# Layer 3's row scales of a four-layer GNN stack, made wholly on GpSimd instead of on VectorE and GpSimd

## The chip, the cores and the metric

The kernel runs on one core of a Trainium2 chip. The metric is the device time of one launch in microseconds (us). Engine names in the profile: PE is TensorE (matmul), PEld its weight loads, DVE is VectorE, ACT is ScalarE, POOL is GpSimd, SP is SyncE, which issues the output DMAs.

## The reference, cut to what matters

Four residual layers run over a batch of 128 graphs of 128 nodes with 64 features: `x = x + layer(relu(layernorm(x)))`, each with its own graph network. The change lies where layer 2's output is folded into `x` and layer 3 begins.

```python
def _layernorm(x, axis=-1, eps=1e-5):
    m = jnp.mean(x, axis=axis, keepdims=True)
    v = jnp.var(x, axis=axis, keepdims=True)
    return (x - m) / jnp.sqrt(v + eps)
...
# end of layer 2: y is normalised over all nodes, then
y = ((y - mean) / jnp.sqrt(var + BN_EPS) * gamma + beta) * m
return jax.nn.relu(y)
...
# layer 3
h = jnp.maximum(_layernorm(x, axis=-1), 0.0)
messages = jnp.einsum('bij,bjh->bih', adjacency, h)
node_in = jnp.concatenate([h, messages], axis=-1)
dh = jnp.tanh(node_in @ W1 + b1) @ W2 + b2
x = x + dh
```

What the change touches is the layernorm of layer 3: for each node and graph, the inverse root of its variance (`rstd`) and the negative mean times it (`nmr`).

## The kernel before, in words

Nodes lie on the 128 partitions and graphs with their features on the free axis, so `x_all` and `y` (a part of `work`) are 128 x 8192 in float32 and stay in SBUF. Layer 0 is the long part of the run (about the first 1000 us), then layer 1 (to about 1220 us), layer 2 (to about 1277 us), and a block that begins with layer 2's batch normalisation (to about 1322 us). The last piece of that block, from about 1322 us to the end, is the fold: layer 2's result is added to `x` while layer 3 already runs over it. The change lies only there.

**Chunks.** The fold cuts `y` and `x` into NXC = 16 chunks of 8 graphs (128 x 512). For each chunk VectorE multiplies `y` by a row vector (`scale_chunk`, L1472), GpSimd adds `beta` (`shift_chunk`, L1477, called the shift below), ScalarE applies the masked relu graph by graph (`masked_relu`, L1599, eight activations in two halves), and VectorE adds it to `x` (L1483) and takes `bn_stats` of each of the eight graphs (L280, both in `add_to_x`).

**Batches.** The layernorm scales are made for QC = 3 chunks at a time, 24 columns; there are NB = 6 batches, the last of one chunk (8 columns). For each batch VectorE makes the variances (`variances`, L1498 to L1506, six instructions), GpSimd raises them to the power of minus a half (L1534), and VectorE corrects that estimate by one Newton step and makes `nmr` (`scales`, L1514 to L1520, four instructions). ScalarE waits for `nmr` of a batch before it normalises the first graphs of it (`norm_group`).

**Layer 3.** It runs over NI = 16 iterations i of two units u = 0 and 1, each of four graphs; a unit is written (i, u) below. Iteration i covers the eight graphs of chunk i. ScalarE normalises four graphs (L1146, `norm_group`, one iteration ahead), TensorE multiplies by the adjacency and transposes (`neighbours`, L1662 and L1666), VectorE copies the sums out of PSUM (L1552, `copy_sums`), TensorE makes the hidden layer (`hidden`, L1672 and L1673), ScalarE the tanh (L1622), TensorE the product (`product`, L1681), VectorE adds the bias to `x` and then the product (L1557 and L1562, `update`), and SP stores the result.

**Order.** Every engine's order is written out by hand. VectorE in iteration i: copy (i, 1), update (i-1, 1), `add_to_x` of chunk i+5, scales of a batch if it is their turn, variances of a batch if its last chunk has just been added, copy (i+1, 0), update (i, 0), `scale_chunk` of chunk i+8. ScalarE in iteration i, unit u: `norm_group` (i+1, u), tanh (i, u), half of the masked relu of chunk i+6. TensorE in iteration i: neighbours (i, 1), hidden (i, 0), product (i-1, 1), neighbours (i+1, 0), hidden (i, 1), product (i, 0). GpSimd: shifts 0 to 4, the power of batch 0, shifts 5 to 7, then for each batch k from 1 its power and the shifts 3k+5 to 3k+7, as far as there are chunks. Five chunks are added before layer 3's first copy, so that batch 0 (chunks 0 to 2) is made ahead of the loop, and the last chunk of batch k is added in iteration 3k-3. Batch k's `nmr` is first read in ScalarE's iteration 3k-1.

Of the kernel before, what the change touches and what calls it, by code (L numbers as in the profile page):

```python
# [7 lines left out]
ALU = mybir.AluOpType  # L8
# [4 lines left out]
def gnn_stack_kernel(nc, a, out):  # L13
# [12 lines left out]
    B, N, F = a["x"].shape  # L26
# [15 lines left out]
    EPS = 1e-5  # L42
    KEY = 257.0
    XC = 512
    NXC = B * F // XC
# [3 lines left out]
    with ctx:  # L49
        def sb(name, shape, dt=F32):  # L50
            return ctx.enter_context(nc.sbuf_tensor(name, shape, dt))

        def sem(name):
            return ctx.enter_context(nc.semaphore(name))
# [52 lines left out]
        var = sb("var", [N, B])  # L107
        dif = sb("dif", [N, B])
        msum = sb("msum", [N, B])
        std = sb("std", [N, B])  # L110
        rstd = sb("rstd", [N, B])
        nmr = sb("nmr", [N, B])
# [1038 lines left out]
        def grp(u, i):  # L1151
            return 2 * i + u
# [280 lines left out]
        s_bn2 = sem("layer3_stats_made")  # L1433
# [9 lines left out]
        s_lnq = sem("l3_scales_step")  # L1443
        s_ln3 = sem("l3_scales_ready")
        s_minus = sem("minus_half_set")
        s_root = sem("inverse_root_estimated")
        LEAD = 6
        QC = 3
        NB = (NXC + QC - 1) // QC
        minus_half = sb("minus_half", [N, QC * GX])  # L1450
# [19 lines left out]
        def scale_chunk(c):  # L1470

            nc.vector.tensor_tensor(g3(yc(c)), g3(yc(c)), per_feature(stat[:, 5, :]), ALU.mult).then_inc(s_ya, 1)  # L1472

        def shift_chunk(pool, c):

            pool.wait_ge(s_ya, c + 1)
            nc.gpsimd.tensor_tensor(g3(yc(c)), g3(yc(c)), per_feature(beta[:, :]), ALU.add).then_inc(s_yb, 1)  # L1477

        def add_to_x(dve, c):

            v = nc.vector
            dve.wait_ge(s_yc, 2 * c + 2)
            v.tensor_tensor(xc(c), xc(c), yc(c), ALU.add).then_inc(s_xn, 1)  # L1483
            dve.wait_ge(s_xn, c + 1)
            for e in range(GX):
                last = stats(c * GX + e)
            last.then_inc(s_bn2, 1)

        def batch(k):
            return slice(k * QC * GX, min((k + 1) * QC, NXC) * GX)  # L1490

        def variances(dve, k):

            v = nc.vector
            cols = batch(k)
            m0, q0, m1, q1 = (bn6[:, cols, t] for t in (1, 2, 4, 5))
            dve.wait_ge(s_bn2, min(QC * k + QC, NXC))
            v.tensor_tensor(msum[:, cols], m0, m1, ALU.add)  # L1498
            v.tensor_tensor(var[:, cols], q0, q1, ALU.add)
            v.tensor_tensor(dif[:, cols], m0, m1, ALU.subtract).then_inc(s_lnq, 1)  # L1500
            dve.wait_ge(s_lnq, 6 * k + 1)
            v.tensor_scalar(var[:, cols], var[:, cols], 1.0 / F, EPS, ALU.mult, ALU.add)
            v.scalar_tensor_tensor(out=dif[:, cols], in0=dif[:, cols], scalar=0.25, in1=dif[:, cols],
                                   op0=ALU.mult, op1=ALU.mult).then_inc(s_lnq, 1)
            dve.wait_ge(s_lnq, 6 * k + 2)
            v.tensor_tensor(var[:, cols], var[:, cols], dif[:, cols], ALU.add).then_inc(s_lnq, 1)  # L1506

        def scales(dve, k):

            v = nc.vector  # L1510
            cols = batch(k)
            root, error = std[:, cols], dif[:, cols]
            dve.wait_ge(s_root, k + 1)
            v.scalar_tensor_tensor(out=error, in0=root, scalar=-0.5, in1=root, op0=ALU.mult, op1=ALU.mult)             .then_inc(s_lnq, 1)  # L1514
            dve.wait_ge(s_lnq, 6 * k + 4)
            v.tensor_tensor(error, error, var[:, cols], ALU.mult).then_inc(s_lnq, 1)
            dve.wait_ge(s_lnq, 6 * k + 5)
            v.scalar_tensor_tensor(out=rstd[:, cols], in0=error, scalar=1.5, in1=root, op0=ALU.add, op1=ALU.mult)             .then_inc(s_lnq, 1)
            dve.wait_ge(s_lnq, 6 * k + 6)
            v.scalar_tensor_tensor(out=nmr[:, cols], in0=msum[:, cols], scalar=-0.5, in1=rstd[:, cols],  # L1520
                                   op0=ALU.mult, op1=ALU.mult).then_inc(s_ln3, 1)

        def shifts_and_roots(pool):

            g = nc.gpsimd

            def shifts(first, past):
                for c in range(first, past):
                    shift_chunk(pool, c)

            def inverse_root(k):
                cols = batch(k)
                pool.wait_ge(s_lnq, 6 * k + 3)
                g.tensor_tensor(std[:, cols], var[:, cols], minus_half[:, 0:cols.stop - cols.start], ALU.pow)\  # L1534
                 .then_inc(s_root, 1)

            g.memset(minus_half[:, :], -0.5).then_inc(s_minus, 1)
            pool.wait_ge(s_minus, 1)
            shifts(0, LEAD - 1)
            inverse_root(0)  # L1540
            shifts(LEAD - 1, LEAD + 2)
            for k in range(1, NB):
                inverse_root(k)
                shifts(min(QC * k + LEAD - 1, NXC), min(QC * k + QC + LEAD - 1, NXC))

        def fold_in(dve):

            v = nc.vector

            def copy_sums(i, u):  # L1550
                dve.wait_ge(s_agg3[u], i + 1)
                v.tensor_copy(msg[:, u, :], bank[4 * u][:, :]).then_inc(s_aggs3[u], 1)  # L1552

            def update(i, u):
                if i > 0:
                    dve.wait_ge(s_out[u], 16 * i)
                v.tensor_tensor(upd[:, u, :].rearrange("p (q f) -> p q f", q=GS),  # L1557
                                x[:, ds(GS * grp(u, i) * F, GS * F)].rearrange("p (q f) -> p q f", q=GS),
                                l3b2[:, :].unsqueeze(1).broadcast_to([N, GS, F]), ALU.add).then_inc(s_xb[u], 1)
                dve.wait_ge(s_dh[u], i + 1)  # L1560
                dve.wait_ge(s_xb[u], i + 1)
                v.tensor_tensor(upd[:, u, :], bank[4 * u + 2][:, 0:GS * F], upd[:, u, :], ALU.add)\  # L1562
                 .then_inc(s_new[u], 1)

            for c in range(3):
                scale_chunk(c)
            for c in range(LEAD - 1):
                add_to_x(dve, c)
                if c == QC - 1:
                    variances(dve, 0)  # L1570
                if c + 3 <= LEAD + 1:
                    scale_chunk(c + 3)
            scales(dve, 0)
            copy_sums(0, 0)
            for i in range(NI):
                copy_sums(i, 1)
                if i > 0:
                    update(i - 1, 1)
                if i + LEAD - 1 < NXC:
                    add_to_x(dve, i + LEAD - 1)  # L1580
                if (i + 2) % QC == 0 and (i + 2) // QC < NB:
                    scales(dve, (i + 2) // QC)
                last = i + LEAD - 1
                if last == NXC - 1 or (last < NXC and last % QC == QC - 1):
                    variances(dve, last // QC)
                if i + 1 < NI:
                    copy_sums(i + 1, 0)
                update(i, 0)
                if i + LEAD + 2 < NXC:
                    scale_chunk(i + LEAD + 2)  # L1590
            update(NI - 1, 1)
# [47 lines left out]
        with nc.Block() as block:  # L1639
# [102 lines left out]
            @block.gpsimd  # L1742
            def _(pool):
                g = nc.gpsimd

                g.memset(block_mask, 1.0).then_inc(s_cutmask, 1)
                pool.wait_ge(s_cutmask, 1)
                g.affine_select(out=block_mask, in_=block_mask, compare_op=ALU.is_ge, fill=0.0,
                                base=0, pattern=[[1, XC]], channel_multiplier=-F).then_inc(s_cutmask, 1)
                pool.wait_ge(s_cutmask, 2)  # L1750
                g.affine_select(out=block_mask, in_=block_mask, compare_op=ALU.is_ge, fill=0.0,
                                base=F - 1, pattern=[[-1, XC]], channel_multiplier=F).then_inc(s_cutmask, 1)
                pool.wait_ge(s_vb, 2)
                normalise(pool, g, 1)
                pool.wait_ge(s_mean, 1)
                centre(pool, g, 1)
                shifts_and_roots(pool)

            @block.sync
            def _(sp):  # L1760
# [34 lines left out]
```

## Time and profile before

| | |
|---|---|
| median of 3 runs | 1448.39 us (1444.45 to 1448.88) |
| profiled execution, its own time | 1445.43 us |
| its span | 1443.7 us, so 1.7 us lie outside |
| PE busy | 1321.2 us (92%) |
| DVE busy | 1162.4 us (81%) |
| ACT busy | 1100.8 us (76%) |
| POOL busy | 510.4 us (35%) |
| mean granted TensorE clock | 0.977 |

The times in the rows are counted from the start of the span. The shares are means over five different stages; only the last 122 us of the span hold work that the change touches.

### The profile page before, as it was taken

What the parts mean: (1) busy time and instruction counts of PE and PEld (TensorE: products, weight loads), DVE (VectorE), ACT (ScalarE), POOL (GpSimd) and SP (SyncE); (2) the same over time, 40 slices, a digit from 0 to 9 for tenths busy, and PEclk for the clock granted to TensorE, in tenths of its full rate; (3) what the DMA queues carried; (4) which work ended last, traced back from release to release, by engine and by line L of the source; (5) the groups of instructions that cost most, each with busy time, mean ns of one, the idle gap of its engine ahead of it and who ended that gap; (6) DMA issues with size and microseconds to landing.
All of it is one profiled execution on the core that took longest, in us unless ns stands there. A gap on an engine that the chain in (4) does not pass through costs nothing. (4 is left out here: it accounts for less than half of the span.)

```text
span 1443.7 us, 40799 instructions
## 1 busy us (share of the span) xinstructions
PE 1321.2 (92%) x11243; PEld 1076.3 (75%) x11244; DVE 1162.4 (81%) x2949; ACT 1100.8 (76%) x2427; POOL 510.4 (35%) x610
## 2 busy tenths in 40 slices
PE   3999999999999999999999999997999998974688
PEld 1777778777787777787777877776988897930677
DVE  8898998889988898888988889886444454977896
ACT  4788888888888888888888888874555554925785
POOL 1333444434444334444344443432212221035441
PEclk9999999999999999999999999999999998987799
DMA  7000000000000000000000000000000000000012
GB/s 154 21 13 9 8 7 14 7 7 7 7 15 7 7 7 7 15 7 7 7 7 15 7 7 7 0 2 1 0 0 0 0 0 0 0 1 0 20 43 55
DMA packets 40928, 18.13 MB, mean 13 GB/s; under 512 B 19573, under 2 KB 40887, under 8 KB 40887
## 3 DMA queue, kind: packets, MB, share of 16 engines
q1 hardware_dynamic: 40354, 17.42, 4.9%
q8 instruction: 19, 0.31, 0.1%
q10 hardware_dynamic: 532, 0.21, 0.1%
q14 instruction: 23, 0.18, 0.0%
HBM read 13.44 MB, written 4.19 MB: 12 GB/s over the span
## 5 line engine op out<-in xcount | busy, mean ns | idle before, releaser
L724 DVE SCALAR_TENSOR_TENSOR acc<-slot_banks,acc 128x768 f32<-128x768 f32 x512 | 487.7, 952 | 77.5 <-PE slot_banks L443 68.3
L793 POOL TENSOR_TENSOR acc<-acc 128x384 f32<-128x384 f32 x128 | 128.0, 1000 | 529.6 <-DVE onediff L718 423.8
L443 PE MATMUL slot_banks<-ac_hi,work 128*128 128x192 f16 x1408 | 265.1, 247 | 27.6 <-DVE work L706 26.7
L443 PE MATMUL slot_banks<-ac_lo,work 128*128 128x192 f16 x1408 | 263.9, 246 | 0.0
L443 PEld LDWEIGHTS slot_banks<-ac_hi,work 128*128 (+1 forms) x1408 | 137.2, 97 | 98.8 <-issue 76.7
L443 PE MATMUL slot_banks<-ac_hi,onediff 128*128 128x192 f16 x1024 | 183.1, 246 | 6.9 <-DVE acc L724 5.1
L443 PE MATMUL slot_banks<-ac_lo,onediff 128*128 128x192 f16 x1024 | 182.4, 246 | 0.0
L443 PEld LDWEIGHTS slot_banks<-ac_lo,work 128*128 (+1 forms) x1408 | 138.0, 98 | 20.3 <-issue 14.5
L779 POOL TENSOR_TENSOR ac_lo<-ac,ac_hi 128x384 f16<-128x384 f32 x128 | 122.7, 959 | 49.4 <-ACT ac_hi L583 49.4
L543 ACT ACTIVATE work<-bank 128x512 f16<-128x512 f32 x256 | 130.5, 601 | 1.2 <-PE bank L354 1.2
L706 DVE TENSOR_SCALAR work<-work,slot_key 128x1024 f16 x256 | 118.0, 480 | 12.3 <-issue 3.7
L582 ACT ACTIVATE ac<-bank 128x384 f32<-128x384 f32 x128 | 62.1, 486 | 81.0 <-PE bank L403 81.0
L591 ACT ACTIVATE acc<-ac,neg_pad 128x768 f32<-128x768 f32 x128 | 119.3, 932 | 0.0
L443 PEld LDWEIGHTS slot_banks<-ac_hi,onediff 128*128 x1024 | 104.7, 102 | 17.1 <-issue 15.3
L607 ACT ACTIVATE slot_banks<-ac 128x768 f32<-128x768 f32 x127 | 103.5, 815 | 11.6
L403 PE MATMUL bank<-wac,hT 65*128 65x384 f32 x256 | 109.5, 510 | 1.7 <-ACT ac_hi L583 1.1
L600 ACT ACTIVATE work<-slot_banks 128x576 f32<-128x576 f32 x128 | 83.3, 651 | 34.9 <-PE slot_banks L443 33.3
L1146 ACT ACTIVATE onediff<-x_all,nmr,rstd 128x64 f32<-128x64 f32 (+1 forms) x256 | 90.7, 430 | 17.8 <-DVE nmr L1520 9.7
L1227 POOL TENSOR_TENSOR adjT_all<-adjT_all,ident 128x512 f32 x32 | 39.9, 1268 | 173.8 <-PE slot_banks L1179 173.8
L443 PEld LDWEIGHTS slot_banks<-ac_lo,onediff 128*128 x1024 | 100.3, 98 | 0.0
L718 DVE TENSOR_TENSOR onediff<-work x128 | 88.6, 692 | 7.4 <-DVE work L706 0.6
L436 PE MATMUL slot_banks<-ac_hi,ident 128*128 128x384 f16 x258 | 85.1, 330 | 0.9 <-issue 0.7
(272 smaller groups left out, 3311.0 us busy)
## 6 DMA issues: line engine op xcount, KB each, us to landing
adj_in<-in_adj_dram SPq DMA_DIRECT2D x32, 256.0 KB, 2.8
out_dram<-acc SPq DMA_DIRECT2D x32, 128.0 KB, 2.0
l1w<-in_L_gnn_W_dram SPq DMA_DIRECT2D x2, 64.0 KB
l1b<-in_L_gnn_b_dram SPq DMA_DIRECT2D x2, 64.0 KB
x_all<-in_x_dram SPq DMA_DIRECT2D x4, 0.2 KB, 11.7
nm_in<-in_nodemask_dram ACTq DMA_DIRECT2D x1, 64.0 KB
w1a<-in_L_gnn_W_dram ACTq DMA_DIRECT2D x1, 48.0 KB
w1b<-in_L_gnn_W_dram ACTq DMA_DIRECT2D x1, 48.0 KB
```

The source lines that it names most:

```text
L403: nc.tensor.matmul(pAC[:, 0:2 * H], hT0[:, p, q * N:(q + 1) * N], wac[:, :], start=True, stop=True)\
L436: nc.tensor.matmul(unit(pair, t, n), node, part[:, q, 0:H].unsqueeze(1).broadcast_to([N, n, H]), start=(e == 0), stop=False)
L443: last = nc.tensor.matmul(unit(pair, t, 1), hot(t), part[:, q, H:2 * H].unsqueeze(1), start=False, stop=(e == 1 and (t % SB == SB - 1 or t ...
L543: last = nc.scalar.activation(rs[:, p, :, t, :], pA3[:, :].rearrange("p (q j) -> p q j", q=GS), ACT.Copy, bias=-float(t))
L591: nc.scalar.activation(acc[:, q, :].rearrange("p (t h) -> p t h", t=SU), ac32[:, q, 0:H].unsqueeze(1).broadcast_to([N, SU, H]), ACT.Relu, ...
L607: nc.scalar.activation(unit((q + 1) % 2, 0, SU), ac32[:, q, 0:H].unsqueeze(1).broadcast_to([N, SU, H]), ACT.Copy).then_inc(s_seed, 1)
L706: nc.vector.tensor_scalar(onehot[:, ds(at, CH)], ranks.rearrange("p t j -> p (t j)"), slot_key[:, ds(key, 1)], None, ALU.is_equal).then_in ...
L718: nc.vector.tensor_tensor(onediff[:, ds(at, CH)], onehot[:, ds(at, CH)], onehot[:, ds(at_old, CH)], ALU.subtract).then_inc(s_D, 1)
L724: nc.vector.scalar_tensor_tensor(out=sums, in0=unit((q + k) % 2, 0, SU), scalar=0.0, in1=sums, op0=ALU.min, op1=ALU.add).then_inc(s_free[k ...
L779: nc.gpsimd.tensor_tensor(ac_lo[:, q, :], ac32[:, q, :], ac_hi[:, q, :], ALU.subtract)\
L793: nc.gpsimd.tensor_tensor(acc[:, q, 0:2 * H], acc[:, q, 0:2 * H], acc[:, q, 2 * H:4 * H], ALU.add)
L1146: ins = nc.scalar.activation(hn[:, u, SLOT[q] * F:(SLOT[q] + 1) * F], x[:, ds((b + q) * F, F)], ACT.Relu, bias=nmr[:, ds(b + q, 1)], scale ...
```

## The change

VectorE no longer makes variances and scales. GpSimd makes all of it in one chain, in the place in its order where the power stood: it waits for the statistics of the batch's last chunk, and issues 14 instructions instead of one, in ten steps with a semaphore wait between them. The correction is written without three-operand instructions, which is why ten VectorE instructions become thirteen on GpSimd beside the power. The shifts keep their places behind it.

```diff
-        def variances(dve, k):
...
-        def scales(dve, k):
...
+        def scales(pool, k):
+
+            g = nc.gpsimd
             cols = batch(k)
+            count = cols.stop - cols.start
             m0, q0, m1, q1 = (bn6[:, cols, t] for t in (1, 2, 4, 5))
             root, error = std[:, cols], dif[:, cols]
+            pool.wait_ge(s_bn2, min(QC * k + QC, NXC))
+            g.tensor_tensor(error, m0, m1, ALU.subtract)
+            g.tensor_tensor(var[:, cols], q0, q1, ALU.add)
+            g.tensor_tensor(msum[:, cols], m0, m1, ALU.add).then_inc(s_lnq, 1)
+            pool.wait_ge(s_lnq, 8 * k + 1)
+            g.tensor_tensor(error, error, error, ALU.mult)
+            g.tensor_scalar(var[:, cols], var[:, cols], 1.0 / F, EPS, ALU.mult, ALU.add)
+            g.tensor_scalar(msum[:, cols], msum[:, cols], -0.5, None, ALU.mult).then_inc(s_lnq, 1)
+            pool.wait_ge(s_lnq, 8 * k + 2)
+            g.tensor_scalar(error, error, 0.25, None, ALU.mult).then_inc(s_lnq, 1)
+            pool.wait_ge(s_lnq, 8 * k + 3)
+            g.tensor_tensor(var[:, cols], var[:, cols], error, ALU.add).then_inc(s_lnq, 1)
+            pool.wait_ge(s_lnq, 8 * k + 4)
+            g.tensor_tensor(root, var[:, cols], minus_half[:, 0:count], ALU.pow).then_inc(s_lnq, 1)
+            pool.wait_ge(s_lnq, 8 * k + 5)
+            g.tensor_tensor(error, root, root, ALU.mult).then_inc(s_lnq, 1)
+            pool.wait_ge(s_lnq, 8 * k + 6)
+            g.tensor_tensor(error, error, var[:, cols], ALU.mult).then_inc(s_lnq, 1)
+            pool.wait_ge(s_lnq, 8 * k + 7)
+            g.tensor_scalar(error, error, -0.5, 1.5, ALU.mult, ALU.add).then_inc(s_lnq, 1)
+            pool.wait_ge(s_lnq, 8 * k + 8)
+            g.tensor_tensor(rstd[:, cols], root, error, ALU.mult).then_inc(s_rs3, 1)
+            pool.wait_ge(s_rs3, k + 1)
+            g.tensor_tensor(nmr[:, cols], msum[:, cols], rstd[:, cols], ALU.mult).then_inc(s_ln3, 1)
...
             shifts(0, LEAD - 1)
-            inverse_root(0)
+            scales(pool, 0)
             shifts(LEAD - 1, LEAD + 2)
             for k in range(1, NB):
-                inverse_root(k)
+                scales(pool, k)
                 shifts(min(QC * k + LEAD - 1, NXC), min(QC * k + QC + LEAD - 1, NXC))
...
             for c in range(LEAD - 1):
                 add_to_x(dve, c)
-                if c == QC - 1:
-                    variances(dve, 0)
                 if c + 3 <= LEAD + 1:
                     scale_chunk(c + 3)
-            scales(dve, 0)
             copy_sums(0, 0)
...
                 if i + LEAD - 1 < NXC:
                     add_to_x(dve, i + LEAD - 1)
-                if (i + 2) % QC == 0 and (i + 2) // QC < NB:
-                    scales(dve, (i + 2) // QC)
-                last = i + LEAD - 1
-                if last == NXC - 1 or (last < NXC and last % QC == QC - 1):
-                    variances(dve, last // QC)
```

## Rows read from the trace of the kernel before

**Rows 1.** Windows: stretch and length; busy PE, PEld, DVE, ACT, POOL; clock; DMA
```profile
1372.00:1391.10 19.10, 16.12 (x110) 14.21 (x108) 18.15 (x58) 16.29 (x55) 7.96 (x4) 1.00 0.19 42
1418.00:1437.60 19.60, 19.60 (x147) 18.75 (x146) 12.51 (x30) 13.27 (x37) 0.00 (x0) 1.00 0.27 60
```

**Rows 2.** Chain of work that ended last: where it leaves VectorE
```profile
1416.60 0.70 PE slot_banks L1672 x2
```

**Rows 3.** VectorE timeline, head: start us, us, line, operation, output and inputs
```profile
1333.02 1.11 DVE L280 BATCH_NORM_STATS2 bn<-x_all 128x6 f32<-128x64 f32 x8
...
1340.35 1.28 DVE L1514 SCALAR_TENSOR_TENSOR dif<-std 128x24 f32<-128x24 f32 x1
...
1344.10 0.18 DVE L1520 SCALAR_TENSOR_TENSOR nmr<-msum,rstd 128x24 f32<-128x24 f32 x1
```

**Rows 4.** VectorE timeline, from batch 1's last chunk to batch 4's
```profile
1351.79 1.11 DVE L280 BATCH_NORM_STATS2 bn<-x_all 128x6 f32<-128x64 f32 x8
...
1370.88 1.11 DVE L280 BATCH_NORM_STATS2 bn<-x_all 128x6 f32<-128x64 f32 x8
1372.02 0.20 DVE L1498 TENSOR_TENSOR msum<-bn 128x24 f32<-128x24 f32 x1
...
1372.88 0.68 DVE L1552 COPY adj_in<-slot_banks 128x512 f32<-128x512 f32 x1
1373.47 0.41 DVE L1557 TENSOR_TENSOR acc<-x_all,l3b 128x256 f32<-128x256 f32 x1
...
1378.14 0.34 DVE L1514 SCALAR_TENSOR_TENSOR dif<-std 128x24 f32<-128x24 f32 x1
...
1379.06 0.68 DVE L1552 COPY adj_in<-slot_banks 128x512 f32<-128x512 f32 x1
...
1381.71 1.12 DVE L1557 TENSOR_TENSOR acc<-x_all,l3b 128x256 f32<-128x256 f32 x1
...
1389.97 1.11 DVE L280 BATCH_NORM_STATS2 bn<-x_all 128x6 f32<-128x64 f32 x8
...
1407.73 1.11 DVE L280 BATCH_NORM_STATS2 bn<-x_all 128x6 f32<-128x64 f32 x8
```

**Rows 5.** ScalarE timeline: norm groups of four graphs, and what they waited for
```profile
1352.80 1.42 ACT L1146 ACTIVATE onediff<-x_all,nmr,rstd 128x64 f32<-128x64 f32 x4
...
1355.43 1.44 ACT L1146 ACTIVATE onediff<-x_all,nmr,rstd 128x64 f32<-128x64 f32 x4
...
1379.23 1.43 ACT L1146 ACTIVATE onediff<-x_all,nmr,rstd 128x64 f32<-128x64 f32 x4 [0.39 <-DVE nmr L1520]
```

**Rows 6.** GpSimd timeline: powers of 24 and 8 columns, and one shift
```profile
1335.19 4.60 POOL L1534 TENSOR_TENSOR std<-var,minus_half 128x24 f32<-128x24 f32 x1 [1.08 <-DVE var L1506]
...
1373.04 4.17 POOL L1534 TENSOR_TENSOR std<-var,minus_half 128x24 f32<-128x24 f32 x1 [3.61 <-DVE var L1506]
...
1381.28 1.28 POOL L1477 TENSOR_TENSOR work<-work,beta 128x512 f32<-128x512 f32 x1 [2.83 <-DVE work L1472]
...
1416.02 1.64 POOL L1534 TENSOR_TENSOR std<-var,minus_half 128x8 f32<-128x8 f32 x1 [1.94 <-DVE var L1506]
```

**Rows 7.** GpSimd groups by shape: count, busy us, mean ns, idle us before
```profile
L793 POOL TENSOR_TENSOR acc<-acc 128x384 f32<-128x384 f32 x128 | 128.0, 1000 | 529.6 <-DVE onediff L718 423.8 <-ACT work L600 105.8
...
L797 POOL TENSOR_TENSOR hm<-work 128x192 f32<-128x192 f32 x128 | 76.9, 601 | 10.0
L795 POOL TENSOR_TENSOR work<-work 128x192 f32<-128x192 f32 x128 | 75.9, 593 | 0.0
...
L1537 POOL MEMSET minus_half<- 128x24 f32 x1 | 0.1, 117 | 0.0
```

**Rows 8.** TensorE timeline, iteration 11: neighbours (12, 0), product, next neighbours
```profile
1418.01 1.06 PE L1662 MATMUL slot_banks<-adjT_all,onediff 128*128 x8
...
1419.99 0.61 PE L1681 MATMUL slot_banks<-l3w,acc 128*128 128x128 f32 x4
1420.43 1.06 PE L1662 MATMUL bank<-adjT_all,onediff 128*128 x8
```

More of the change, by code:

```diff
@@ L1445, in gnn_stack_kernel @@
         s_minus = sem("minus_half_set")
-        s_root = sem("inverse_root_estimated")
+        s_rs3 = sem("l3_inverse_roots_ready")
         LEAD = 6
@@ L1490, in batch @@
             return slice(k * QC * GX, min((k + 1) * QC, NXC) * GX)
-        def variances(dve, k):
-            v = nc.vector
+        def scales(pool, k):
+            g = nc.gpsimd
             cols = batch(k)
+            count = cols.stop - cols.start
             m0, q0, m1, q1 = (bn6[:, cols, t] for t in (1, 2, 4, 5))
[L1497 to L1506, printed above, removed]
@@ L1508, in scales @@
-        def scales(dve, k):
-            v = nc.vector
-            cols = batch(k)
-            root, error = std[:, cols], dif[:, cols]
[L1513 to L1521, printed above, removed]
@@ L1523, in shifts_and_roots @@
-        def shifts_and_roots(pool):
+            root, error = std[:, cols], dif[:, cols]
+            pool.wait_ge(s_bn2, min(QC * k + QC, NXC))
[5 more added lines that the diff above has]
+            g.tensor_scalar(var[:, cols], var[:, cols], 1.0 / F, EPS, ALU.mult, ALU.add)
@@ L1525, in shifts_and_roots, with shifts_and_scales @@
+            pool.wait_ge(s_rs3, k + 1)
+            g.tensor_tensor(nmr[:, cols], msum[:, cols], rstd[:, cols], ALU.mult).then_inc(s_ln3, 1)
+        def shifts_and_scales(pool):
             g = nc.gpsimd
@@ L1529, in shifts @@
                     shift_chunk(pool, c)
[L1531 to L1535, printed above, removed]
             g.memset(minus_half[:, :], -0.5).then_inc(s_minus, 1)
@@ L1756, in _ @@
                 centre(pool, g, 1)
-                shifts_and_roots(pool)
+                shifts_and_scales(pool)
             @block.sync
```

## The prediction

> **What bounds the kernel now.** I read the windows of the fold first, to see which engine fills each stretch. While chunks are still being added, VectorE is busy 18.15 of 19.10 us, ahead of ScalarE (16.29) and TensorE (16.12). Once the chunks are done, TensorE fills 19.60 of 19.60 us and VectorE has a third of its time free [rows 1]. The chain of waits agrees: it runs down VectorE alone for some 60 us and changes to TensorE at 1416.60 [rows 2]. So only what VectorE does before that point can be worth time, and what it does behind it is free.
>
> The VectorE timeline gives the rhythm. I call T(k) the end of `bn_stats` of batch k's last chunk (start plus duration), where the batch's scales can begin: 1333.02 + 1.11 = 1334.13 for batch 0 [rows 3], then 1352.90, 1371.99, 1391.08 and 1408.84 [rows 4]. The periods are 19.09, 19.09 and 17.76 us. N(k) is the end of `nmr`. N(0) is 1344.28 [rows 3], so L(0) = N(0) - T(0) = 10.15 us; for batch 2, ScalarE waits 0.39 us for `nmr` and starts at 1379.23, so L(2) is about 7.1 us [rows 5]. `nmr` is already slightly late before the change. That is why I treat this as a question of latency as much as of work.
>
> **What is removed.** Per batch, variances take VectorE from 1371.99 to the next copy at 1372.88, 0.89 us, and scales from 1378.14 to 1379.06, 0.9 us [rows 4]. Ten instructions, 1.8 us per batch with issue gaps. The scales of batch 0 lie ahead of the loop where ScalarE waits for them, those of batch 5 behind 1416.60 where VectorE has time. VectorE's floor for a period becomes 19.09 - 1.8 = 17.3 us, of which 1.4 us is something else: twice per period L1557 takes 1.12 instead of 0.41 us (1381.71, five such in the fold) [rows 4], each time with a shift of 1.28 us running on GpSimd, that one from 1381.28 to 1382.56 [rows 6]. No DMA is issued or moved; SP's queue still waits on the same updates.
>
> **What is added.** Per batch GpSimd gets 13 instructions of 24 columns beside the power. The trace has no such instruction. Two groups of the same operation give a line: 1.000 us for 384 columns, 0.593 for 192, so 2.12 ns a column and 0.19 us fixed, 0.235 us at 24 columns [rows 7]. Bounds: below, the memset of 24 columns, 0.117 us, which reads nothing [rows 7]; above, the power, which took 4.17 us for 24 and 1.64 for 8 columns [rows 6], so 0.37 us fixed, and 0.42 us with 24 columns at 2.12 ns. I take 0.235, since it is the same kind of instruction, and keep both ends. A wait for GpSimd's own last result costs 10.0 us / 128 = 0.08 us (L797 follows L795 in that way) [rows 7].
>
> The chain undisturbed: 0.09 to start; two steps of three instructions, 2 x (0.2 + 0.2 + 0.235 + 0.08) = 1.43; two single steps, 2 x 0.315 = 0.63; the power, 4.17 + 0.08; four steps, 1.26; the last, 0.235. Sum 7.9 us. On top comes VectorE. The power of batch 0 took 4.60 instead of 4.17 us, started at 1335.19 beside a two-input VectorE instruction [rows 6], so a GpSimd instruction can wait for such a one. In a batch's first 3 us VectorE runs L1557 and L1472, in its last 1.5 us another L1557: 0.34 + 0.6 + 0.34, about 1.2 us. **L = 9.1 us**, against 7.1 before. It gets longer by 2 us, though VectorE gets shorter.
>
> **What the latency sets.** From N(k) the way to T(k+1), step by step: ScalarE's next unit starts one ScalarE period later, 1355.43 - 1352.80 = 2.63, its four activations take 1.43 [rows 5]: 4.1. TensorE needs 1.98 for neighbours and hidden and 0.44 for the product [rows 8]: 6.55. VectorE then ends update (0.42), adds the chunk to `x` (0.61) and takes statistics (1.11, rows 4): R = 8.8 us with three hand-overs of 0.03. (In the head the trace shows it directly: 1344.28 to 1352.90, 8.6 us.) Add 0.15 because shift 3k+7 now falls on the L1557 before it. So a period is the longer of L + 8.95 and VectorE's own 17.3 us plus 0.3 for more collisions. At L = 9.1 it is 18.05: **the loop through GpSimd becomes the bound**, just over VectorE's 17.6.
>
> **The sum.**
> - Head: the 24-column chain runs beside two L1472 and two L1483, 0.6 us each, with its small steps: 7.9 + 2.2 = 10.1 us, against 10.15. Before, three of the four instructions of scales took 1.2 to 1.3 us each beside the shifts (L1514, 1.28, rows 3); that stall goes, and others take its place. -0.1.
> - Periods T(1) to T(2) and T(2) to T(3): 18.05 - 19.09 = -1.04 each.
> - T(3) to T(4): 17.9 (no shift 3k+7 any more) against 17.76: +0.1.
> - End: neighbours (12, 0) started at 1418.01, 9.17 us after T(4) [rows 8]. After: L(4) = 8.6 (no L1472 beside it) plus 1.5 for the norm group, 10.1: +1.0. From there TensorE is full to the end in both.
> Sum -1.1 us. The profiled execution took 1445.43 us (span 1443.7 and 1.7 around it), 3.0 below the median of 1448.39. It would be 1444.3; the four times known have their middle at 1446.9, 1.5 above the profiled one, so I forecast **1446 us** for a median. Two periods pay, the end takes it back.
>
> What hides the rest: shift 3k+5 waits behind the chain from about T + 2 to T + 9.1 and is done 1.3 us after N(k); ScalarE wants it 1.43 + 0.47 = 1.9 us after N(k). Cover 0.6 us. Behind it in GpSimd's queue wait only the next shifts, each wanted one iteration, some 5 us, later. If a VectorE instruction delays it by its 0.6 us, the cover is gone and ScalarE starts to lose, under 0.5 us a batch. Batch 5's chain (8 columns, power 1.64) is wanted ten microseconds later and costs nothing.
>
> **A rule against it.** During the power, from 1373.04, VectorE's two-input L1557 took its normal 0.41 us [rows 4, 6], while beside shifts it took 1.12: so the first row suggests that a GpSimd instruction holds VectorE back only while it moves data. The Trainium skill (SBUF — State Buffer, Who interferes with whom) has it otherwise: the pair of ports is locked for the whole instruction and the loser blocks fully. By that rule every one of the small instructions could hold VectorE, and the power too; the shift's row agrees with it, the power's doesn't, and by the rule the sum would be that of the third rival below.
>
> **The rivals.** Everything hangs on d, the time of a small GpSimd instruction. It enters five links (head, three periods, end), 13 times each, so 0.1 us more is 6.5 us.
> - **GpSimd's chain is too long: slower.** At d = 0.42 L is 11.5 and the sum -1.1 + 65 x 0.185 = +10.9, 1457 us. It is slower by over 0.3% (4.3 us, about what a measurement of this kernel can tell) from d = 0.32 on. For it: the power's fixed part, and one power already waited. Against: the line through two plain groups. 0.22.
> - **The chain is short and VectorE stays the bound: faster.** If collisions cost GpSimd little or d is 0.15, L is 7 to 8: head -2, periods -1.6, -1.6 and -1, end -0.5, together -6.7: 1440 us. For it: VectorE's load in rows 1. 0.22.
> - **VectorE is held by the small instructions.** Four of its two-input instructions per batch wait up to 0.235 each: 17.3 + 1.0 = 18.3 a period instead of 18.05, +0.25 twice and a little at the end: 1447 us. 0.16.
> - **Nothing it does reaches the end** (batches are made early enough, or shifts late to the same measure): 1447 us. 0.05.
> My forecast keeps 0.35. So faster 0.22, same 0.56, slower 0.22. The range 1440 to 1456 takes in the faster case's middle and d up to about 0.38.
>
> **What would show it.** Right: GpSimd's small instructions at 0.2 to 0.27 us; `nmr` 9 us after T(k) in batches 1 to 3; ScalarE waiting for GpSimd's `nmr` about 1 to 2 us in each of batches 1 to 4; periods near 18 us; VectorE with 1 us idle per period; neighbours (12, 0) some 10 us after T(4). Wrong: small instructions over 0.32 us with periods over 19 us, or no wait of ScalarE for `nmr` and VectorE full as before.

## The result, and the profile after

The changed kernel takes 1452.78 us (median of 8 runs, 1451.28 to 1455.57) against 1448.26 us for the kernel before (8 runs): ratio 1.0042, 95% interval 1.0031 to 1.0054. The ratio is taken over all runs, here and below; the two medians alone give 1.0031. Either way it is slower, by 4.5 to 6 us. The forecast was 1446 us and no change; the time lies inside the range of 1440 to 1456, the direction does not.

The profiled execution took a span of 1450.4 us against 1443.7. T(0) comes 1.5 us later (1335.66 against 1334.13), ahead of anything that the change touches; I count that as spread between executions. (In the eleven profiled executions with this lead, whose code up to T(0) is the same, it lies between 1334.1 and 1337.8.) The other 5.2 us lie in the fold.

The page's chain that ended last, by engine and by line. GpSimd was at 0% before and now stands ahead of VectorE, with the power at its head:
```profile
PE 5%; POOL 3%; DVE 2%; ACT 1%; issue 0%; DMA 0%; DVEq 0%; SPq 0%; ACTq 0%; POOLq 0%
POOL std L1512 1%; PE slot_banks L1638 1%; PE slot_banks L1631 1%; PE slot_banks L1649 1%; PE bank L1649 1%; DVE bn L280 1%; ACT onediff L1146 0%; DVE x_all L1483 0%; PE slot_banks L1668 0%; PE bank L1660 0%; PE bank L1659 0%; PE bank L1668 0%; PE slot_banks L1659 0%; PE slot_banks L1660 0%; POOL var L1505 0%
```

Windows of the kernel after (columns as in [rows 1]): the period T(2) to T(3), and the end. VectorE is down from 18.15 to 15.32 us of work: 1.4 us of it is that the two L1557 that took 1.12 us each ([rows 4]) take 0.41 to 0.46 here, where no shift runs beside them, and the rest is the instructions moved. Nothing else fills the longer period of 20.2 us; the granted TensorE clock in it is 0.92 instead of 1.00:
```profile
1373.60:1393.80 20.20, 17.27 (x112) 15.78 (x110) 15.32 (x50) 16.24 (x55) 12.30 (x17) 0.92 0.18 39
1428.00:1444.00 16.00, 16.00 (x120) 15.28 (x119) 9.71 (x20) 9.84 (x28) 0.00 (x0) 1.00 0.26 58
```

GpSimd timeline of batch 2. A small instruction starts 0.21 us after the one before it in the first step, 0.28 to 0.30 us in the second (0.30 from L1504 to L1505), and 0.31 us after it or a little more where it waits for it; 0.54, 0.70 and 0.75 us are those that came beside a two-input VectorE instruction. This is the row kind that [rows 7] had only at 192 and 384 columns:
```profile
1373.72 0.26 POOL L1500 TENSOR_TENSOR dif<-bn 128x24 f32<-128x24 f32 x1 [2.63 <-DVE bn L280]
1373.93 0.25 POOL L1501 TENSOR_TENSOR var<-bn 128x24 f32<-128x24 f32 x1
1374.14 0.54 POOL L1502 TENSOR_TENSOR msum<-bn 128x24 f32<-128x24 f32 x1
1374.76 0.23 POOL L1504 TENSOR_TENSOR dif<-dif 128x24 f32<-128x24 f32 x1
1375.06 0.70 POOL L1505 TENSOR_SCALAR var<-var 128x24 f32<-128x24 f32 x1
...
1376.85 4.20 POOL L1512 TENSOR_TENSOR std<-var,minus_half 128x24 f32<-128x24 f32 x1
1381.12 0.23 POOL L1514 TENSOR_TENSOR dif<-std 128x24 f32<-128x24 f32 x1
...
1382.41 0.75 POOL L1522 TENSOR_TENSOR nmr<-msum,rstd 128x24 f32<-128x24 f32 x1
1383.13 2.48 POOL L1477 TENSOR_TENSOR work<-work,beta 128x512 f32<-128x512 f32 x2
```

ScalarE timeline: the four norm groups that wait for a batch (0.39 us was the wait of batch 2 before, [rows 5]):
```profile
1364.38 1.44 ACT L1146 ACTIVATE onediff<-x_all,nmr,rstd 128x64 f32<-128x64 f32 x4 [1.95 <-POOL nmr L1522]
...
1383.26 1.44 ACT L1146 ACTIVATE onediff<-x_all,nmr,rstd 128x64 f32<-128x64 f32 x4 [2.86 <-POOL nmr L1522]
...
1403.44 1.44 ACT L1146 ACTIVATE onediff<-x_all,nmr,rstd 128x64 f32<-128x64 f32 x4 [2.84 <-POOL nmr L1522]
...
1421.30 1.43 ACT L1146 ACTIVATE onediff<-x_all,nmr,rstd 128x64 f32<-128x64 f32 x4 [2.90 <-POOL nmr L1522]
```

VectorE timeline, the rows that answer to [rows 3] and [rows 4]: the statistics that end at T(0) to T(4), and a copy that VectorE now waits 2.05 us for:
```profile
1334.55 1.11 DVE L280 BATCH_NORM_STATS2 bn<-x_all 128x6 f32<-128x64 f32 x8
...
1353.39 1.11 DVE L280 BATCH_NORM_STATS2 bn<-x_all 128x6 f32<-128x64 f32 x8
...
1372.53 1.11 DVE L280 BATCH_NORM_STATS2 bn<-x_all 128x6 f32<-128x64 f32 x8
...
1386.27 0.69 DVE L1547 COPY adj_in<-slot_banks 128x512 f32<-128x512 f32 x1 [2.05 <-PE slot_banks L1653]
...
1392.71 1.11 DVE L280 BATCH_NORM_STATS2 bn<-x_all 128x6 f32<-128x64 f32 x8
...
1411.48 1.11 DVE L280 BATCH_NORM_STATS2 bn<-x_all 128x6 f32<-128x64 f32 x8
```

TensorE timeline, neighbours (12, 0), which was at 1418.01 with 1.06 us in [rows 8]:
```profile
1422.90 1.27 PE L1649 MATMUL slot_banks<-adjT_all,onediff 128*128 x8 [2.15 <-ACT onediff L1146]
```
The neighbours that waited for batches 2 and 3:
```profile
1384.87 1.15 PE L1649 MATMUL slot_banks<-adjT_all,onediff 128*128 x8 [2.93 <-ACT onediff L1146]
...
1405.05 1.15 PE L1649 MATMUL slot_banks<-adjT_all,onediff 128*128 x8 [2.92 <-ACT onediff L1146]
```

And two short windows behind the waits of batches 2 and 4. TensorE is busy throughout and its granted clock is 0.66 and 0.50: for much of the first and all of the second it runs at 1.2 instead of 2.4 GHz.
```profile
1385.00:1389.00 4.00, 4.00 (x21) 3.68 (x22) 1.32 (x3) 3.51 (x14) 0.61 (x1) 0.66 0.00 0
1424.00:1427.00 3.00, 3.00 (x12) 2.65 (x11) 1.02 (x2) 1.09 (x4) 2.16 (x6) 0.50 0.00 0
```

With the prediction's own quantities (L(k) from T(k) to the end of `nmr`, R(k) from there to T(k+1)):

| piece | before | after | forecast of the difference | measured |
|---|---|---|---|---|
| T(0) to T(1) | 18.77 | 18.84 (L 10.21, R 8.63) | -0.1 | +0.07 |
| T(1) to T(2) | 19.09 | 19.14 (L 9.48, R 9.66) | -1.04 | +0.05 |
| T(2) to T(3) | 19.09 | 20.18 (L 9.52, R 10.66) | -1.04 | +1.09 |
| T(3) to T(4) | 17.76 | 18.77 (L 9.53, R 9.24) | +0.1 | +1.01 |
| T(4) to neighbours (12, 0) | 9.17 | 10.31 | +1.0 | +1.14 |
| from there to the end of the span | 25.7 | 27.5 | 0 | +1.8 |
| sum | | | -1.1 | +5.2 |

### The profile page after: what moved, and what is told of

The parts are those of the page before. It is cut to its first block and busy times, and to the rows that moved or that the text cites. A ratio compares the mean times of both kernels' runs of the same rounds, so it can differ in the third digit from the quotient of the medians.

```text
span 1450.4 us, 40817 instructions
## 1 busy us (share of the span) xinstructions
PE 1324.6 (91%) x11243; PEld 1080.2 (74%) x11244; DVE 1148.8 (79%) x2889; ACT 1102.7 (76%) x2427; POOL 534.7 (37%) x688
## 5 line engine op out<-in xcount | busy, mean ns | idle before, releaser
L443 PEld LDWEIGHTS slot_banks<-ac_lo,work 128*128 (+1 forms) x1408 | 138.1, 98 | 20.2 <-issue 14.5
L607 ACT ACTIVATE slot_banks<-ac 128x768 f32<-128x768 f32 x127 | 103.6, 816 | 11.6
L1146 ACT ACTIVATE onediff<-x_all,nmr,rstd 128x64 f32<-128x64 f32 (+1 forms) x256 | 91.5, 434 | 26.4 <-POOL nmr L1522 18.8
```

Of the source, the lines that this page charges most:

```text
L443: last = nc.tensor.matmul(unit(pair, t, 1), hot(t), part[:, q, H:2 * H].unsqueeze(1), start=False, stop=(e == 1 and (t % SB == SB - 1 or t ...
L607: nc.scalar.activation(unit((q + 1) % 2, 0, SU), ac32[:, q, 0:H].unsqueeze(1).broadcast_to([N, SU, H]), ACT.Copy).then_inc(s_seed, 1)
L1146: ins = nc.scalar.activation(hn[:, u, SLOT[q] * F:(SLOT[q] + 1) * F], x[:, ds((b + q) * F, F)], ACT.Relu, bias=nmr[:, ds(b + q, 1)], scale ...
```

## The experiments

Ratios are to the kernel before, run on the same chips, with the 95% interval. The runs lie on several chips, where the kernel before itself has medians from 1445.9 to 1448.3 us, so a difference between the medians of two runs is good to 2 us at best. Periods, waits and clocks are those of the one profiled execution of each run. Theory 1: what the chain costs is latency, along T(k), `nmr`, ScalarE, TensorE, VectorE, T(k+1). Theory 2: the many small GpSimd instructions hold VectorE up. Theory C came with the windows above: after the waits the TensorE clock falls, and that costs time of its own.

**1. The latency taken away, the work kept.** GpSimd's results go to other tiles, and ScalarE normalises layer 3 with the scales left from layer 2: the batch's own scales are made but not used.
```diff
-            g.tensor_tensor(rstd[:, cols], root, error, ALU.mult).then_inc(s_rs3, 1)
+            g.tensor_tensor(error, root, error, ALU.mult).then_inc(s_rs3, 1)
...
-            g.tensor_tensor(nmr[:, cols], msum[:, cols], rstd[:, cols], ALU.mult).then_inc(s_ln3, 1)
+            g.tensor_tensor(ss[:, cols], msum[:, cols], error, ALU.mult).then_inc(s_ln3, 1)
...
-                    act.wait_ge(s_ln3, i // QC + 1)
+                    act.wait_ge(s_bn2, min(QC * (i // QC) + QC, NXC))
```


> The changed kernel with ScalarE reading layer 2's old rstd and nmr and waiting only for the batch's statistics; GpSimd still does all its 14 instructions per batch, into other tiles. So the work and its collisions stay and only the latency is gone; layer 3 is normalised with the wrong scales. Theory 1 (the way T(k) -> nmr -> ScalarE -> TensorE -> VectorE -> T(k+1) is what costs): periods fall from 19.1, 20.2 and 18.8 us to VectorE's floor of 16.5 to 17.6, neighbours (12, 0) starts 7 to 8 us after T(4) instead of 10.3, no stretch at half the TensorE clock, and the time is 8 to 13 us below the changed kernel, about 1441 us. Theory 2 (the many small GpSimd instructions hold VectorE up): VectorE's two-input instructions stay longer than 0.41 and 0.68 us and the periods stay above 18 us; the time stays within 3 us of 1452.

Measured: 1447.95 us, 1.0007 (0.9996 to 1.0019). Half of what I expected, and by the periods neither theory held: 21.4, 19.9 and 19.8 us. ScalarE's timeline says why. It passes the norm group and the tanh and then stands at the masked relu, whose shift is queued on GpSimd behind the chain:
```profile
1377.85 1.42 ACT L1146 ACTIVATE onediff<-x_all,nmr,rstd 128x64 f32<-128x64 f32 x4
1379.18 0.47 ACT L1609 ACTIVATE acc<-slot_banks,l3b 128x256 f32<-128x256 f32 x1
1382.87 1.06 ACT L1586 ACTIVATE work<-work,nm 128x64 f32<-128x64 f32 x4 [3.21 <-POOL work L1477]
```
The latency has two ways to ScalarE, nearly equally long. I had seen the second one only as a cover of 0.6 us. TensorE waited 3.30 and 2.45 us behind these two waits (to 1385.43 and 1405.32), and its clock fell after both, which I had said it would not: 0.59 granted from 1385 to 1389 us, 0.65 from 1405 to 1409.

**2. Both ways cut.** As 1, and the first shift goes ahead of the chain.
```diff
-                scales(pool, k)
-                shifts(min(QC * k + LEAD - 1, NXC), min(QC * k + QC + LEAD - 1, NXC))
+                first, past = min(QC * k + LEAD - 1, NXC), min(QC * k + QC + LEAD - 1, NXC)
+                shifts(first, min(first + 1, past))
+                scales(pool, k)
+                shifts(min(first + 1, past), past)
```


> As the first of the nowait runs (wrong scales read, no wait for nmr), but GpSimd does shift 3k+5 ahead of batch k's chain instead of behind it. Theory 1a (what the chain costs is latency, and it reaches ScalarE by two ways, nmr and the shift queued behind the chain): with both gone, ScalarE waits neither for nmr nor for a shift, the periods fall from 19.8 to 21.4 us to VectorE's 17 to 18, and the time is 5 to 8 us below the nowait run, 1440 to 1443 us. Theory 2 (the GpSimd work itself slows VectorE): periods stay above 19 us and the time within 2 us of 1448.

Measured: 1440.46 us, 0.9947 (0.9930 to 0.9963). All of ScalarE's waits between 1350 and 1425 us are now short ones for TensorE:
```profile
ACT acc L1611 <- PE slot_banks L1662: 4.9, 7, 1.2
ACT acc L1611 <- PE bank L1662: 3.7, 4, 1.7
```
GpSimd did the same 14 instructions per batch, and the time is some 7 us below the kernel before, so theory 2 falls: what the changed kernel loses, this and 6 us more, goes by the latency and by the clock that falls behind it. How much of the 7 us is the work moved and how much the waits that the kernel before has too stays open, since no run takes the waits out of that kernel. The period T(2) to T(3) is 17.9 us here, with VectorE busy 17.2 (I had 17.6 for its floor), and T(3) to T(4) is 16.0. T(1) to T(2) did not fall as expected; it is 21.3 us. There TensorE had waited 5.09 us (to 1350.35), behind the shift that stands after batch 0's chain, and its clock had fallen:
```profile
1351.05:1372.35 21.30, 21.17 (x135) 19.19 (x134) 17.18 (x50) 19.52 (x68) 11.75 (x17) 0.90 0.17 37
```

**3. The chain made longer.** Four more multiplications of 24 columns ahead of `nmr`, written to a tile that nobody reads.
```diff
+            for e in range(4):
+                g.tensor_tensor(ss[:, cols], msum[:, cols], rstd[:, cols], ALU.mult).then_inc(s_pad, 1)
+                pool.wait_ge(s_pad, 4 * k + e + 1)
             g.tensor_tensor(nmr[:, cols], msum[:, cols], rstd[:, cols], ALU.mult).then_inc(s_ln3, 1)
```


> The changed kernel with four more 24-column multiplications in each chain, one after the other ahead of nmr: 4 x 0.32 = 1.3 us more latency and hardly more work for the shared reads. Theory 1 (every period and the end are set by the chain's latency): head, three periods and the end get 1.3 us each, so 5 to 7 us above the changed kernel, 1458 to 1460 us. Theory 2 (work, not latency): under 2 us more, 1453 to 1455.

Measured: 1462.71 us, 1.0103 (1.0086 to 1.0120), 9.9 us above the changed kernel by the medians, 8.8 by the ratios. More than five links of 1.3 us. In the profiled executions the spans differ by 10.8 us. Of this the five L have 6.8 (each grows by 1.2 to 1.7 us); R(1) to R(3) are 11.3, 10.8 and 11.6 instead of 9.7, 10.7 and 9.2 and have 4.1. TensorE's timeline behind batch 2's wait shows the reason: eight matmuls that take 1.06 us in [rows 8] take 2.07.
```profile
1390.56 2.07 PE L1653 MATMUL slot_banks<-adjT_all,onediff 128*128 x8 [4.50 <-ACT onediff L1146]
```
In this run the clock fell after every batch. Theory C gains weight.

**4 and 5. TensorE's loop written out, and then kept busy.** The first is the control. In the second 16 matmuls that nobody reads stand ahead of neighbours (3k, 0).
```diff
-                pairs(pe, pair)
+                for i in range(NI):
+                    pair(i)
...
+                        if u == 1 and i in (2, 5, 8, 11):
+                            for _ in range(16):
+                                nc.tensor.matmul(bank[3][:, 0:N], ident[:, :], ident[:, :], start=True, stop=True)
```


> The changed kernel with TensorE's loop over layer 3 written out, nothing else: the control for the next run. Expected within 1.5 us of the changed kernel's 1452.8.

> The same, with 16 matmuls of 128x128 (about 1.75 us) that nobody reads ahead of neighbours (3k, 0), where TensorE waits 2 to 3 us for the late nmr of batches 1 to 4. Theory C (the granted TensorE clock falls to half after that wait and costs 1.2 us after batch 2 and 1.8 us after batch 4): the windows at 1385 to 1389 and 1424 to 1427 show full clock, and the time is 2 to 4 us below the control. Without theory C: within 1 us of the control, or above it.

Measured: 1451.14 us, 1.0029 (1.0018 to 1.0039) for the control; 1452.10 us, 1.0030 (1.0018 to 1.0042) with the matmuls. No gain. The clock was kept through the loop (1.00 from 1354 to 1440 us), but the filler was too long: each of these float32 matmuls stands as two in the trace, and 16 took 3.74 us, against a wait of 2 to 3.
```profile
1384.10 3.74 PE L1677 MATMUL slot_banks<-ident 128*128 128x128 f32 x32
1387.68 1.06 PE L1649 MATMUL slot_banks<-adjT_all,onediff 128*128 128x128 f32 x8
```

**6. The same with 11 matmuls, for batches 2 to 4 alone** (`range(11)`, `i in (5, 8, 11)`).

> The run with matmuls that nobody reads again, now 11 instead of 16 and only in iterations 5, 8 and 11. Each had two passes and 16 took 3.7 us, longer than the wait of 2.8 us, so that they delayed neighbours (3k, 0) by 0.3 us and more and gave back what the kept clock brought. 11 take 2.4 us and fit in the wait. Theory C (the fall of the clock after the wait costs 1.2 to 1.8 us each time that it happens, two times in the changed kernel): full clock in all windows of the loop, 2 to 3 us below the 1451.1 of the written-out control, 1448 to 1449.5 us. If theory C is only a side effect: within 1 us of 1451.

Measured: 1448.33 us, 1.0015 (1.0003 to 1.0028), 2.8 us below the control by the medians and 2.0 by the ratios. The two intervals overlap (1.0018 to 1.0028), so by the times alone the gain is likely but not certain. The windows say more. The control at half clock behind two batches:
```profile
1404.00:1410.00 6.00, 4.61 (x22) 4.33 (x23) 2.12 (x10) 4.65 (x16) 2.26 (x2) 0.72 0.11 26
1426.00:1430.00 4.00, 4.00 (x19) 3.72 (x18) 1.42 (x3) 1.98 (x6) 1.77 (x6) 0.58 0.03 8
```
With 11 matmuls, behind batches 1 (no filler), 2 and 4:
```profile
1364.00:1368.00 4.00, 2.68 (x11) 2.61 (x12) 2.49 (x10) 3.90 (x13) 2.34 (x2) 0.67 0.16 35
1384.00:1389.00 5.00, 4.38 (x34) 3.94 (x33) 2.74 (x13) 4.75 (x16) 2.60 (x3) 1.00 0.12 26
1421.00:1427.00 6.00, 6.00 (x47) 5.73 (x47) 2.07 (x5) 4.92 (x14) 4.32 (x14) 1.00 0.13 29
```
Its period T(3) to T(4) is 18.65 us against the control's 20.07, and its T(1) to T(2), where the clock fell, is 20.6 us against 18.9. The changed kernel and the control differ in the same way: behind batch 2, after waits of 2.93 and 2.86 us, R is 10.66 with the fall and 9.23 without; behind batch 3, after 2.92 and 2.86 us, it is 9.24 without and 10.55 with it. So one fall costs 1.3 to 1.7 us, and theory C holds by the periods.

**7. Only the variances back on VectorE.** Seven VectorE instructions; GpSimd keeps the power, the correction and `nmr`.
```diff
+        def variances(dve, k):
...
+            v.tensor_scalar(msum[:, cols], msum[:, cols], -0.5, None, ALU.mult)
...
         def scales(pool, k):
...
-            pool.wait_ge(s_bn2, min(QC * k + QC, NXC))
...
+            pool.wait_ge(s_lnv, 3 * k + 3)
             g.tensor_tensor(root, var[:, cols], minus_half[:, 0:count], ALU.pow).then_inc(s_lnq, 1)
```


> The variances go back to VectorE (7 instructions, about 0.95 us a batch); GpSimd keeps the power, the correction and nmr. Theory 1: nmr comes 0.95 + 0.1 + 4.2 + 0.08 + 1.5 = 6.8 us after T(k), and 6.8 + 9.3 is 16.1, under VectorE's floor of about 17.5 to 18, so VectorE bounds again; periods 17.5 to 18, and the time is 3 to 6 us below the kernel before, about 1444 us. Theory 2: five small GpSimd instructions instead of 13 remove only part of the collisions, and the time lies midway between the two kernels or above, 1448 to 1451 us.

Measured: 1443.09 us, 0.9975 (0.9965 to 0.9986). As theory 1 has it: L is 6.9 us, and ScalarE waits for `nmr` only in batch 4 (1.24 us). Periods are 18.8, 19.4 and 17.5 us, longer than I expected, with VectorE busy 17.95, 18.18 and 16.66 of them. In the second of them the TensorE clock had fallen as well, after a wait of only 1.55 us (to 1373.60). The kernel before has a wait of 1.48 us at the same place, and its clock stayed at 1.00:
```profile
1371.89:1391.30 19.41, 17.47 (x110) 15.57 (x108) 18.18 (x55) 16.20 (x55) 9.15 (x9) 0.91 0.19 41
```
Six of its L1557 and two of its L1473 are held to 1.1 us and more, here by two shifts (GpSimd's timeline, then VectorE's):
```profile
1362.11 1.27 POOL L1478 TENSOR_TENSOR work<-work,beta 128x512 f32<-128x512 f32 x1 [0.63 <-DVE work L1473]
...
1368.07 1.27 POOL L1478 TENSOR_TENSOR work<-work,beta 128x512 f32<-128x512 f32 x1 [4.68 <-DVE work L1473]
```
```profile
1362.56 1.11 DVE L1557 TENSOR_TENSOR acc<-x_all,l3b 128x256 f32<-128x256 f32 x1
...
1368.51 1.11 DVE L1557 TENSOR_TENSOR acc<-x_all,l3b 128x256 f32<-128x256 f32 x1
```

**8. The other half.** GpSimd makes the variances (seven instructions) and the power, VectorE the correction in iteration 3k-2 as before. The edit is against the kernel before.
```diff
...
             def inverse_root(k):
                 cols = batch(k)
-                pool.wait_ge(s_lnq, 6 * k + 3)
+                variances(pool, k)
+                pool.wait_ge(s_lnv, 4 * k + 4)
```


> The other half: GpSimd makes the variances and the power, VectorE the correction and nmr in iteration 3k-2 as before. The power ends 2.5 + 0.6 + 4.2 = 7.2 us after T(k), VectorE's correction 0.8 us later at the soonest: nmr at 8.0 to 8.5 us after T(k). Theory 1: latency of 8.3 + 9.3 = 17.6 a period, about VectorE's floor of 16 + 0.9 + collisions 1.8 = 18.7 us; time near the kernel before, 1445 to 1449 us, and worse than the run with the variances on VectorE (0.9975 of before). Theory 2 (number of small GpSimd instructions): 7 of 13, midway to the changed kernel, 1449 to 1451.

Measured: 1457.06 us, 1.0069 (1.0051 to 1.0087), the worst split of all and a miss of both theories. VectorE now waits itself, with its copies queued behind, and then loses another 1 us to the shift that GpSimd starts at that moment (VectorE's timeline, then GpSimd's):
```profile
1384.01 1.23 DVE L1516 SCALAR_TENSOR_TENSOR dif<-std 128x24 f32<-128x24 f32 x1 [2.13 <-POOL std L1537]
```
```profile
1379.78 4.20 POOL L1537 TENSOR_TENSOR std<-var,minus_half 128x24 f32<-128x24 f32 x1
1383.94 1.26 POOL L1478 TENSOR_TENSOR work<-work,beta 128x512 f32<-128x512 f32 x1
```
I had taken the power's end (7.4 us after T(2)) for a matter of ScalarE alone and forgotten who stands in VectorE's queue. TensorE waited 3.82 and 3.09 us behind batches 2 and 3, and its clock fell after both (0.50 from 1386 to 1392 us, 0.61 from 1410 to 1414). No run separates the three costs.

**9 to 11. One more chunk of lead** (`LEAD = 7`), in the changed kernel, in the kernel before, and in 7. In the last two a call of `variances(dve, 1)` is added ahead of the loop, and in the kernel before the last batch's variances keep their iteration.

> The changed kernel with seven instead of six chunks of lead, so that each batch's statistics are ready one iteration (5.3 us) before the point where they are now, with the same GpSimd work. Theory 1: T(k) to ScalarE's need grows from 7 to about 12 us, above the 9.5 us that the chain takes, so no wait for nmr in the loop and periods at VectorE's floor of about 17; the head gets 1.5 to 2.5 us longer by one shift ahead of the first chain, the loop has one chunk less. Time 5 to 10 us below the changed kernel, 1442 to 1447 us, below the kernel before. Theory 2: the same collisions, time within 3 us of 1452.

> The kernel before with seven chunks of lead, as a control: it is bound by VectorE's work and hardly by latency, so theory 1 expects little, between 2 us less (one chunk fewer inside the VectorE-bound loop) and 2 us more (longer head) than the kernel before: 1446 to 1450 us. If it gains as much as the changed kernel does with seven, the lead itself is worth the time and says nothing of the GpSimd chain.

> Variances on VectorE, the rest on GpSimd, and seven chunks of lead. With six chunks this split has already no wait for nmr but the last (1.2 us) and is bound by VectorE (periods 18.8, 19.4, 17.5). One more chunk of lead removes the last wait, takes one chunk out of the VectorE-bound loop and lengthens the head by about 2 us: 1441 to 1444 us, within 2 us of the same split with six (1443.1). If latency still played a part there it would gain 3 us or more.

Measured: 1444.68 us, 0.9982 (0.9971 to 0.9994) on the changed kernel; 1447.95, 1.0003 (0.9991 to 1.0016) on the kernel before; 1445.16, 0.9987 (0.9977 to 0.9998) on 7. The lead is worth 8 us where the chain is late and nothing where it is not. In the changed kernel's loop ScalarE waited for `nmr` four times, 1.95 to 2.90 us each; now it waits twice, 0.28 and 0.48 us, and the clock stays at 1.00 from 1354 us on. On 7 it costs 2 us by the medians, 1 us more than I allowed for, with intervals that overlap: no gain, as is to be expected of a kernel that latency hardly binds.

**12. The shifts moved off L1557.** 7, with `scale_chunk` between the addition to `x` and `bn_stats`.
```diff
             v.tensor_tensor(xc(c), xc(c), yc(c), ALU.add).then_inc(s_xn, 1)
+            if ahead < NXC:
+                scale_chunk(ahead)
...
-                if i + LEAD + 2 < NXC:
-                    scale_chunk(i + LEAD + 2)
```


> Variances on VectorE, power, correction and nmr on GpSimd (as in the run at 0.9975 of before), and VectorE's scale_chunk of chunk i+8 moved from the end of iteration i to between the addition to x and the eight bn_stats of the same iteration. The shift of 1.28 us that it releases on GpSimd then runs beside bn_stats, which have one input each, instead of beside L1557, which has two and was held to 1.1 us seven times in that run's loop. If the rest of VectorE's excess is these collisions (about 5.5 us in all, 3.5 to 5 of it from shifts), periods go from 18.8, 19.4 and 17.5 to 17.2 to 17.8 us, L1557 stays at 0.41 us, and the time is 2 to 4 us lower, 1439 to 1441 us, 0.995 of the kernel before. If something else sets the periods (ScalarE's 15.9 or the latency, 6.9 + 9.3 = 16.2), it gains more than that is not possible and less means that the shifts collide elsewhere: 1443.

Measured: 1437.27 us (5 runs), 0.9947 (0.9933 to 0.9961), 8.7 us below the kernel before by the medians and 7.7 by the ratio, so below both kernels of the comparison, and somewhat below my 1439 to 1441. Periods are 17.1, 17.0 and 16.1 us. Over the three of them VectorE is busy 5.0 us less than in 7 with the same instructions, and they are 5.5 us shorter together. That the shifts only come earlier is no rival: in 7's loop ScalarE never waited for one. The clock is a small rival: it fell once in 7's profiled execution and not in this one, but VectorE was idle only 1.2 us in that period. The group of all 32 L1559 (L1557 before) has no held one left (three additions to `x` in the loop take 1.09 to 1.25 us instead of 0.68), while a shift from 1361.83 to 1363.10 runs beside `bn_stats` and a copy:
```profile
L1559 DVE TENSOR_TENSOR acc<-x_all,l3b 128x256 f32<-128x256 f32 x32 | 13.3, 416 | 0.9 <-DMA out_dram<-acc 0.9
```
```profile
1361.67 1.10 DVE L280 BATCH_NORM_STATS2 bn<-x_all 128x6 f32<-128x64 f32 x8
1362.69 0.67 DVE L1554 COPY adj_in<-slot_banks 128x512 f32<-128x512 f32 x1
```
```profile
1361.83 1.27 POOL L1478 TENSOR_TENSOR work<-work,beta 128x512 f32<-128x512 f32 x1 [1.23 <-DVE work L1473]
```

## Why the prediction was wrong

The mechanism was right, and two terms of its sum were too small: R, the way from `nmr` to the next T, and the end, where TensorE was taken to run at full clock.

- **d, the small instruction: right.** 0.235 us forecast, 0.21 to 0.28 us measured where nothing came between. The line through two wider groups of the same operation was a good source. Its upper end, the power's fixed part, was not needed.
- **L: 9.1 forecast, 9.5 measured** in batches 1 to 3 (8.6 as forecast in batch 4). The part for VectorE was right: three instructions per chain take 0.3 to 0.5 us more beside it, 1.27 us in batch 2 against 1.2. The undisturbed chain was short: 8.25 us instead of 7.9, more than half of the miss in the second step, whose instructions start 0.28 to 0.30 us apart and not 0.2. In batch 4 the two errors cancel (8.3 and one delay of 0.3 instead of 7.9 and 0.6), which is luck. It is 0.4 us in each of three periods.
- **R: the step that failed first.** 8.95 us forecast (8.8 for the last period), 9.66, 10.66 and 9.24 measured. Behind batch 3, at full clock, 0.17 us of the miss is a misreading: I counted 0.44 us for the product, which in [rows 8] is the distance to the next matmul's start, while its own time stands there as 0.61, and VectorE starts 0.64 us after it (1420.63 against 1419.99). I had taken hand-overs at 0.03 us; from ScalarE to TensorE it is 0.16 (norm group to 1384.71, matmul at 1384.87), from `nmr` to ScalarE 0.1, and in batch 1 ScalarE started 0.4 us after `nmr`. And I had taken TensorE's times from a stretch without a wait. The new wait changes them: behind batch 2's the clock fell to half and R grew to 10.66.
- **"From there TensorE is full to the end in both": the step that failed with it.** TensorE was full, but at 1.2 GHz until about 1427, and the last stretch took 27.5 instead of 25.7 us. From neighbours (12, 0) to (12, 1) it is 4.05 us instead of 2.42. Run 6 bears out that the clock is a cost of its own: kept busy in the wait, TensorE keeps it, and 2 to 3 us come back, by intervals that overlap.
- **VectorE's floor of 17.6: nearly right** with the shifts colliding as they did, 17.9 in run 2; run 12 got to 17.0 with more work on VectorE and fewer collisions. It never came into play, since L + R was above it in each period.
- **The shift's cover of 0.6 us: right for the changed kernel** (no wait for a shift in its loop), but run 1 shows that it is the next bound as soon as `nmr` is in time.
- **Port rule.** In the changed kernel VectorE's L1552 took 0.44 to 0.49 us beside the small instructions and 0.42 beside the power, instead of 0.41; it was GpSimd that waited, up to 0.5 us each time in the loop and 1.0 to 1.1 us twice in the head (L1500 took 1.23 us, L1506 1.30). The Trainium skill (SBUF — State Buffer, Who interferes with whom) has it that a VectorE instruction with two SBUF inputs contends with a GpSimd instruction that reads SBUF, and calls contention an exclusive lock; that one side fully blocks for the whole instruction of the other it writes of VectorE's two-port modes, and the prediction read it as holding for both. The shifts agree with that reading (1.11 us in run 7), the power of 4.2 us does not. The third rival, VectorE held by small instructions, is out.

In the sum: the L term is worth 1.2 us of the miss of 6.3, R at full clock about 1.4, the falls of the clock about 3.2 (1.4 in R(2), 1.8 in the last stretch), the rest is the head, the start of (12, 0) and rounding. The slower rival was right in its place (a latency that costs more than the work saved) but not in its price: it put the whole risk on d, and the clock was in none of the cases. Shown by the runs are the latency (1, 2, 3, 9), the second way through the shift (1 and 2) and the clock (by the periods of the changed kernel, 4 and 6; less sharply by 6's time). That the first 1.5 us, before T(0), are spread is argued from the unchanged code and the range of T(0), not tested.

## What to carry to other kernels

Work that leaves the bound engine for an idle, slower one helps only if its result still comes in time: write down who wants it, how long after its input, and compare with the new chain's length before counting what was freed. Look also at what is queued behind the chain on its new engine, since that is the second deadline. Splitting the job so that the chain stays short, and timing the other engine's long instructions beside one-input work, got here what the full move lost: 0.9947 instead of 1.0042.

## What the runs showed of the hardware that was not expected

- After TensorE had waited 2 to 4.5 us for `nmr`, its granted clock stood at half for some 2 to 3 us (0.50 in the window from 1424 to 1427 us), though the engine was busy throughout; with the longer chain 5 us once (0.50 from 1412 to 1417). It did not happen after each such wait: in the changed kernel after batches 2 and 4, not after 1 (2.03 us) and not after 3, whose wait of 2.92 us was as long; in the written-out control after 3 and 4; with the longer chain after every one. In run 7 it came after a wait of 1.55 us. What decides it stays open.
- A GpSimd power of 24 columns (4.2 us) ran beside two-input VectorE instructions without holding them, while a 1.27 us addition of 512 columns held one from 0.41 to 1.11 us.
- Making GpSimd's chain 1.3 us longer cost 9.9 us over five batches (8.8 by the ratios): of the 10.8 us between the profiled spans 6.8 lie in the chains themselves and the rest in R(1) and R(3), in which TensorE now ran at half clock for a time, as it had not before.
